# Neighbour maximum of a graph network: at most two sure gathers under way at a time

## What is computed

```
# layer 0: for each node the largest value of each feature over its neighbours
vals = max over j with adj[i, j] != 0 of X[j, :]        # 0 where a node has none
x = layernorm(x + vals)
# layers 1 to 3: attention over the neighbours
h = x @ W;  e = leaky_relu(h @ a_src + (h @ a_dst).T)
att = softmax(where(adj > 0, e, -big))                   # layer 1 also cuts small values
x = layernorm(x + elu(att @ h (+ h in layer 1)))
```

## Time and profile before

| | us |
|---|---|
| median of 3 runs | 5301.23 (5296.34 to 5317.98) |
| profiled execution, span | 5833.8 |
| neighbour maximum in it | about 2300 |
| granted TensorE clock, mean | 0.934 |

### The profile page before, as it was taken

One profiled execution on the slowest core, in us unless ns is written; L12 is line 12 of the kernel. 1 busy time (PEld: TensorE's weight loads), 2 busy tenths in 40 slices (PEclk: granted clock), 3 DMA queues, 4 the chain that ended last, 5 costly groups with the idle time before them and its releaser, 6 DMA issues. The chain is left out here.

```text
span 5833.8 us, 79888 instructions
## 1 busy us (share of the span) xinstructions
PE 4973.9 (85%) x24050; PEld 2353.4 (40%) x24159; DVE 4815.6 (83%) x8933; ACT 1971.0 (34%) x2773; POOL 1213.0 (21%) x1383
## 2 busy tenths in 40 slices
PE   4777676667677666899999999989999998999999
PEld 3333333333333333344444444434444445444444
DVE  6676666676676677899999999998999996999998
ACT  3444444444444442555555555510000001000000
POOL 5555444454454542000000000000000000000000
PEclk6888888888888887999999999999999998999999
DMA  7555555555555552011111111002222212222211
GB/s 265 187 193 188 184 193 176 186 188 189 184 187 186 178 166 83 30 44 44 44 44 44 44 44 44 30 37 83 81 79 81 77 52 77 80 89 73 97 67 36
DMA packets 153847, 635.17 MB, mean 109 GB/s; under 512 B 29872, under 2 KB 38576, under 8 KB 96112
## 3 DMA queue, kind: packets, MB, share of 16 engines
q1 hardware_dynamic: 82912, 490.51, 24.1%
q0 software_dynamic: 33744, 73.21, 4.2%
q10 hardware_dynamic: 36864, 67.13, 3.3%
HBM read 559.29 MB, written 75.63 MB: 109 GB/s over the span
## 5 line engine op out<-in xcount | busy, mean ns | idle before, releaser
L1388 PE MATMUL bank<-w,GX 128*128 128x512 f32 x6144 | 2762.9, 597 | 20.4 <-DVE w L1640 15.6
L1388 PEld LDWEIGHTS bank<-w,GX 128*128 128x128 f32 x6144 | 1151.1, 190 | 1360.9 <-issue 1310.2
L1656 DVE SCALAR_TENSOR_TENSOR w<-q,E,m 128x512 f32<-128x512 f32 x2048 | 1472.6, 760 | 130.3 <-PE bank L1388 39.1
L376 POOL DMA_INDIRECT ring<-x_ext,idx x1051 | 1030.7, 981 | 1086.9 <-DVE X L637 333.8
L625 DVE TENSOR_TENSOR top<-top,sums 128x1024 f32<-128x1024 f32 x484 | 589.9, 1219 | 639.8 <-remote 375.1
L527 PE MATMUL sums<-lone,xs 128*128 128x512 fp8e4 x3000 | 850.9, 426 | 289.7 <-DVE top L625 195.9
L450 ACT ACTIVATE stage<-tp 128x1024 fp8e4<-128x1024 uint16 x512 | 523.7, 1024 | 1073.3 <-remote 627.8
L1640 DVE SCALAR_TENSOR_TENSOR w<-q,E,u 128x512 f32<-128x512 f32 x1024 | 761.1, 745 | 31.8 <-PE bank L1388 30.5
L1629 DVE SCALAR_TENSOR_TENSOR u<-theta,E,m 128x512 fp8e4<-128x512 f32 x1024 | 766.1, 749 | 8.6 <-DVE w L1640 3.7
L1460 ACT ACTIVATE above<-bank,offset 128x512 fp8e4<-128x512 f32 x932 | 593.2, 683 | 531.5 <-PE bank L1316 531.1
L527 PEld LDWEIGHTS sums<-lone,xs 128*128 128x128 bf16 x3000 | 294.6, 106 | 813.9 <-issue 604.5
(11 more groups left out here) (237 smaller groups left out, 3021.1 us busy)
## 6 DMA issues: line engine op xcount, KB each, us to landing
adjb<-in_adj SPq DMA_DIRECT2D x256, 1024.0 KB
m<-mask_t SPq DMA_DIRECT2D x192, 1024.0 KB, 4.9
mask_t<-stage ACTq DMA_DIRECT2D x256, 256.0 KB
ring<-x_ext,idx POOLq DMA_INDIRECT x1051
z<-row_scores SPq DMA_DIRECT2D x30, 256.0 KB, 5.0
out<-X SPq DMA_DIRECT2D x16, 256.0 KB, 2.4
Wn<-in_L_gnn_W SPq DMA_DIRECT2D x3, 64.0 KB, 1.9
A<-in_L_gnn_a SPq DMA_DIRECT2D x6, 0.5 KB, 2.5
```

What stands on the lines that cost most here:

```text
L376: pool.indirect_dma_start(ring[:, s, :], None, x_ext, bass.IndirectOffsetOnAxis(ap=idx[:, k, s:s + 1], axis=0)).then_inc(done, 16)
L1388: last = nc.tensor.matmul(acc[b][:, :], GX[:, j, :], w[:, j % WR, :], start=(j == 0), stop=(j == T - 1))
L1656: nc.vector.scalar_tensor_tensor(out=w[:, j % WR, :], in0=q, scalar=E[:, j:j + 1], in1=m[:, b, j, :], op0=ALU.max, op1=ALU.mult).then_inc( ...
```

## The change

`gathered` becomes two semaphores. The sure gathers of a tile count on them in turn: the first on `gathered0`, the second on `gathered1`, and so on, six on each. Ahead of each sure gather from the third on, and ahead of the first two gathers of the second group, GpSimd waits until the gather before the last has landed (`landed`). DVE waits for both semaphores where it waited for one.

```
-        gathered = sem("gathered")
+        gathered = [sem("gathered0"), sem("gathered1")]
...
+            def landed(t, n):
+
+                hold(pool, gathered[(n - 1) % 2], (t * (SIZES[0] // 2) + (n + 1) // 2) * 16)
+
...
                 for part in range(2):
                     follow(part)
-                    gather(k, HALF // 2 + 3 * part, 3, gathered)
+                    for i in range(3):
+                        if 3 * part + i >= 2:
+                            landed(t, 3 * part + i - 1)
+                        gather(k, HALF // 2 + 3 * part + i, 1, gathered[(3 * part + i) % 2])
                 report()
                 hold(pool, lower_free, t + 1)
                 for part in range(3):
                     follow(2 + part)
-                    gather(k, 2 * part, 2, gathered)
+                    for i in range(2):
+                        landed(t, HALF // 2 + 2 * part + i - 1)
+                        gather(k, 2 * part + i, 1, gathered[i])
                 hold(pool, rest_free, t + 1)
-                gather(k, FIRST[1], SIZES[1], low_in)
+                for i in range(SIZES[1]):
+                    if i < 2:
+                        landed(t, HALF + i - 1)
+                    gather(k, FIRST[1] + i, 1, low_in)
...
                 if finishes:
-                    hold(dve, gathered, (old + 1) * 16 * SIZES[0])
+                    for number in gathered:
+                        hold(dve, number, (old + 1) * 16 * (SIZES[0] // 2))
                     larger(0, 0, h // 2, h // 2).then_inc(upper_free, 1)
```

## The result

The changed kernel took 5982.3 us (median of 4 runs, 5966.9 to 5990.2) beside 5298.8 us: ratio 1.1286, 95% interval 1.1259 to 1.1314. The way was forecast, the size was not: 683 us lost instead of 268, outside the range of 5285 to 5750.

The account below looks back on a forecast made before the run. DVE was taken to bound the neighbour maximum's tile at 25.4 us, and GpSimd to replace it at 29.8: 4.4 us x 61 tiles = 268 us on 5301, say 5570 us, range 5285 to 5750.

Parts of the forecast that it names:

- The timed tile, 25.4 us: Neighbour maximum: DVE bounds the tile at 25.4 us when timed, 33.9 when profiled, the 532.6 us difference put into 63 tiles.
- the span forecast for the changed profile: Profiled execution of the changed kernel: 5800 to 6000 us, with most of the loss only in the timed runs.
- No cost of the instructions, the order, DVE's second wait: GpSimd's extra instructions cost nothing, gather order stays, DVE's wait for two semaphores costs some tens of ns.
- GpSimd's turn, 29.8 us: GpSimd's whole time per tile in the neighbour maximum: 23.4 us for six pairs of gathers plus 6.4 for the rest.
- p = L + 0.75: Time for two gathers on GpSimd, landing time plus restart: 3.9 us instead of 2.5, between 3.05 and 4.75.
- The restart: On GpSimd, from the release of a waiting gather to its start: 0.75 to 0.8 us, not hidden behind a landing.
- The landing L: Time for a gather to land: 2.3 us free of loads, 4.0 held by one, 3.15 taken.
- a rule that takes a maximum: A gather on GpSimd starts at the later of previous gather plus 1.25 us and last-but-one plus landing plus 0.75.
- Half of the gathers held: Adjacency loads and stores fill about half of the tile, so half of the gathers wait for a load's end.
- C: Far slower: every pair of gathers falls into a load, GpSimd's turn 34.9 us, 5880 us; chance 0.08 for above 5750.
- B: Faster: fewer gathers in flight free PE's reads or signals, shortening DVE's remote waits, at most 116 us, 5185 us; chance 0.08.
- A: No change: loads don't hold gathers in timed runs, or timed tile nearer 30 us; turn 24.7 us, 5301 us; chance 0.17.

Follow-up runs that it names:

- x1: Changed kernel with its 12 new waits a tile on an event already passed, none on a landing: 5824.3 us beside 5819.5 for the kernel before, ratio 1.0013.
- y1: The kernel before the change, unaltered, run again for its trace; it met the lower level: 5298.6 us, ratio 1.0010.
- x7: Changed kernel with adjacency loads of 64 KB in place of 1 MB from tile 1 on: 5471.4 us, ratio 1.033 to the kernel before.
- x9: The kernel before the change, unaltered, run again for its trace; it met the upper level: 5813.2 us, ratio 0.9993.

## Why the prediction was right in direction and wrong in size

**The timed tile, 25.4 us: right.** The trace of the lower level has 25.5. That was luck. The reason given, that profiling makes the difference, was wrong: profiled executions of both levels agree with their medians (5813.4 us beside 5817, 5297.7 beside 5295), the trace ahead of the prediction was of the other level, and the median happened to be of the lower. So was the span forecast for the changed profile: "5800 to 6000" was met, but most of the loss was to show only in timed runs, and the profiled run showed all of it.

**No cost of the instructions, the order, DVE's second wait: right** (x1, 0.1%).

**GpSimd becomes the bound: right** (idle between tiles 0.16 us instead of 4.21, and the time follows the limit).

**GpSimd's turn, 29.8 us: this step failed,** in the term p = L + 0.75 for a pair, 3.9 us predicted and 4.65 measured. Averaged over 55 tiles from the starts of the gathers, the turn was 36.2 us, in three parts:

| term | predicted | measured |
|---|---|---|
| six pairs, first to thirteenth gather | 6 x 3.9 = 23.4 | 6 x 4.65 = 27.9 |
| thirteenth to the tile's last | 1.25 + 1.25 + 1.75 = 4.25 | 5.9 |
| last to the next tile's first | 2.15 | 2.4 |

A pair is landing plus restart. The restart was right: from the update of the semaphore that GpSimd waits for to the start of the gather 0.77 us pass, in 71% of the pairs' first gathers under 0.8; the sum had 0.75, from a gather released by DVE. With a limit of one, where nothing but landing and restart can play, it is 0.80 us on average. Two other things were wrong.

The landing L was read to the wrong end. The prediction took it to the last packet, and so taken it was sized rightly: 3.15 predicted, 3.2 measured (2.35 where nothing met a load, 4.0 where one did). But the wait ends with the semaphore's update, which the trace shows 0.3 us or more behind that packet. Taken to the update the landing is 3.67 us on average and about 2.5 where free: 0.5 us more, six times a tile, 3.1 us.

And I had put averages into a rule that takes a maximum. The later of two times is on average later than either's average: where the gather before had itself been held up, its 1.25 us set the start, long after the own release had come. In the six pairs that is 1.1 us a tile. Both together make 4.2 of the 4.5 us. The rule itself holds: with each gather's own two times ("the one before plus 1.25", "the update plus 0.77") it leaves 0.5 us of a tile open. The second part of the table has the same fault: the fourteenth gather starts by its own chain of pairs, 2.7 us behind the thirteenth on average and not 1.25.

36.0 - 25.5 = 10.5 us over 63 tiles is 662 us of the 683.

**Held or not.** Half of the gathers held was right: 522 of 1051 found at least one of the 16 engines on a load or store when their packets were due (1.65 us behind the start, the soonest that any came). Here too luck helped. The landings had been read in a trace of the upper level, with its long tile. In y1, where the kernel is fast, 834 of 1051 were held and a sure gather took 4.0 us to its last packet, not 3.15: loads are denser in a short tile. The changed kernel's own tile is long again, 36 us, and so its landings are near those of the trace that was read.

**Rivals.** C, far slower, had 0.08 and comes nearest: 5880 us, for a turn of 34.9. Its reason, that every pair falls into step with a load, holds for some of the pairs: the second and third pair of a tile took 5.8 and 5.4 us on average, the fourth and fifth 3.8 and 3.6. The measured pair, 4.65, lies just beyond the 4.4 at which the forecast's own case ended. B, faster, was wrong for this comparison, but its mechanism exists on the other level, where limits of three and four gain 2.6 and 3.5%; it said gathers each 1.25 us apart speak against it, and they don't: by the counts above it matters how many are under way. A fell with y1 (landings of 4.0 us in a fast run) and x7.

By the rule of the Trainium skill (DMA: Bandwidth & Descriptors, queues, rings and completion order) a DMA engine takes turns between the queue rows that have work, packet by packet. The traces don't agree: q0 stood empty for 3.3 us beside a busy q1, gathers that met a load took 4.0 us and not 2.35, and x7 shows that the loads are the cause.

## What to carry to other kernels

A limit on transfers under way costs the engine that issues them (landing + restart)/limit per transfer; set it so that this stays below what the engine needs to issue one: here (3.7 + 0.8)/1.25 = 3.6, so at least four, and only six were free (landings vary, and a load holds several gathers at once). Sum such chains with the maximum of each step, not with averages, and take a landing to the update of the semaphore, not to the last packet. Ask first which level a trace belongs to: compare its own time with the median before drawing anything from the difference.

## What the runs showed of the hardware

The same kernel ran at two levels 10% apart, 5295 and 5817 us, with the same chip at both. At the upper one the engines behind PE began over 1 us late in 0 of 143 cases with no gather under way, 5% with one, 33% with two and 36% with three; at the lower in none of 861. PE's granted clock from 600 to 1200 us was 0.88 there (x9) and 0.99 at the lower (y1). What sets the level is not known. Four gathers at a time is the best limit seen at the upper (5607 us) and costs 1% at the lower; six costs nothing at the lower, and was not run at the upper. The upper level's traces also lack records: two thirds of the updates of the gathers' semaphore in x9.

A gather of 64 KB has its last packet 2.35 us behind its start where it meets no load, and its semaphore's update 0.3 us or more later; 0.77 us behind the update the next waiting gather starts. If a 1 MB load of the hardware queue runs when its packets are due, the gather mostly waits for the load's end: q0 empty for 3.3 us, last packet after 4.0 us on average.
